# Quartered load of x, feed-forward weight scaling in the first attention, and the rotary addition on VectorE, in a two-layer transformer kernel

## The reference

```python
x = x + attn0(layernorm(x))   # 16 heads of 16, causal; rotary positions on q and k
x = x + ffn0(layernorm(x))    # layernorm again, sign(weight) product, then * max|weight| * gamma + beta
x = x + attn1(layernorm(x))   # 16 heads of 128, causal, with biases
x = x + moe(layernorm(x))     # 64 experts, 6 per token, capacity 96, plus a shared expert
```

## Time and profile before

| what | value |
|---|---|
| median of 3 runs | 1561.48 us |
| lowest, highest | 1559.58, 1565.09 us |
| span of the profiled execution, first to last instruction | 1556.1 us |
| busy in the span: PE, DVE, ACT, POOL | 1394.1, 1047.9, 814.5, 374.1 us |
| mean granted TensorE clock | 0.948 of full speed |

### The profile page before, as it was taken

How to read it: one execution, slowest core, us unless ns; L and a number is a source line. 1 busy time by engine, 2 the same in 40 slices (tenths; PEclk the granted TensorE clock), 3 DMA queues, 4 the chain that set the end, 5 groups by cost and what they waited for, 6 DMA issues and landing times. The chain is left out here.

```text
span 1556.1 us, 36410 instructions
## 1 busy us (share of the span) xinstructions
PE 1394.1 (90%) x12869; PEld 982.9 (63%) x12869; DVE 1047.9 (67%) x2191; ACT 814.5 (52%) x1682; POOL 374.1 (24%) x796
## 2 busy tenths in 40 slices
PE   3848999999679999999989999999998798799977
PEld 2414555554556777777777677777767745599963
DVE  4856777764778888888822888888882378422228
ACT  1316665655327877777711877787770116222330
POOL 0434665530021111111110101111101000577730
PEclk9969999999889999999999999999999799799985
DMA  3038999872025655565620665566651430599948
GB/s 101 1 68 170 248 246 248 214 160 52 1 79 113 143 138 138 133 142 133 138 59 1 129 141 134 135 142 138 138 128 31 133 95 1 162 290 288 289 135 295
DMA packets 463401, 215.08 MB, mean 138 GB/s; under 512 B 412082, under 2 KB 434448, under 8 KB 463072
## 3 DMA queue, kind: packets, MB, share of 16 engines
q1 hardware_dynamic: 448992, 175.09, 47.0%
q0 software_dynamic: 12000, 36.90, 8.0%
q10 hardware_dynamic: 2336, 2.16, 0.4%
HBM read 81.97 MB, written 31.52 MB: 73 GB/s over the span
## 5 line engine op out<-in xcount | busy, mean ns | idle before, releaser
L1073 PE MATMUL bank<-a_pt,v_part 128*128 128x128 f16 x3456 | 235.3, 220 | 13.9 <-DMA a_pt<-a_ph 8.9
L1136 ACT ACTIVATE a_ph<-a_p,a_rinv 128x1024 f16<-128x1024 f32 (+7 forms) x256 | 198.7, 777 | 79.3 <-POOL a_rinv L1015 75.7
L755 DVE TENSOR_REDUCE a_qh<-bank 128x1 f16<-128x1024 f32 (+7 forms) x256 | 182.3, 755 | 85.0 <-PE bank L645 83.3
L1073 PEld LDWEIGHTS bank<-a_pt,v_part 128*128 128x128 f16 x3456 | 208.9, 98 | 47.2 <-DVE z_part L1163 7.5
L1144 DVE TENSOR_REDUCE a_negm<-bank 128x1 f32<-128x1024 f32 (+7 forms) x256 | 191.7, 749 | 55.9 <-PE bank L1057 55.7
L1052 PE MATMUL bank<-a_k,a_q 128*128 128x512 f16 (+3 forms) x1152 | 228.7, 326 | 0.2
L743 ACT ACTIVATE a_p<-bank 128x1024 f32<-128x1024 f32 (+7 forms) x256 | 157.8, 649 | 128.7 <-PE bank L700 113.3
L1178 DVE SCALAR_TENSOR_TENSOR a_ph<-a_p,a_rinv,a_ph 128x1024 f16<-128x1024 f32 (+7 forms) x256 | 206.8, 808 | 1.7 <-ACT a_ph L1136 1.7
L1125 ACT ACTIVATE a_p<-bank,a_negm 128x1024 f32<-128x1024 f32 (+7 forms) x256 | 189.3, 739 | 21.6 <-DVE a_negm L1144 21.6
L1015 POOL TENSOR_TENSOR a_rinv<-a_rinv,p_scale 128x1 f32<-128x1 f32 x256 | 48.8, 191 | 610.6 <-DVE a_rinv L1157 610.4
L924 PE MATMUL bank<-x_part,wsplit 128*128 128x512 f16 x768 | 186.0, 379 | 4.1 <-PEq L199 1.8
(11 more groups left out here) (206 smaller groups left out, 2230.9 us busy)
## 6 DMA issues: line engine op xcount, KB each, us to landing
wgu<-in_wgu SPq DMA_DIRECT2D x64, 352.0 KB
choice_rows<-zero POOLq DMA_DIRECT2D x24, 512.0 KB, 4.9
c_rows<-choice_rows SPq DMA_DIRECT2D x16, 768.0 KB, 11.2
wsplit<-w_parts POOLq DMA_DIRECT2D x30, 384.0 KB, 3.8
wd<-in_wd SPq DMA_DIRECT2D x64, 176.0 KB
pw_in<-in_wqkv SPq DMA_DIRECT2D x16, 384.0 KB, 4.9
w_parts<-pw_part SPq DMA_DIRECT2D x16, 384.0 KB, 2.9
a_pt<-a_ph SPq DMA_TRANSPOSE x256, 3.0
```

The costliest lines, as they stand in the source:

```text
L755: dve.tensor_reduce(qh[s][:, i, MC:MC + 1], s1_place(t), AX.X, ALU.max, negate=True).then_inc(m_ready, 1)
L1073: ins = eng.matmul(Z_ps[:, cols], g.vs[par][v_][:, k, :], turned[slot][:, a * blocks[j] + k, :], start=(k == 0 and (v_, a) == PARTS[0]), s ...
L1136: eng.activation(parts[slot][:, 0:w_], probs[slot][:, 0:w_], ACT.Copy, scale=rinv[:, p_, jj:jj + 1]).then_inc(p_hi, 1)
```

## The change

- x is loaded in four transfers of four tiles, each with its own semaphore, and DVE takes the statistics of a quarter's tiles as soon as that quarter has landed, in `load` instead of `norm`.
- The transfers of the attention's and the feed-forward sublayer's weights are issued in `load`, behind those of x; SP waits for them in `norm`.
- POOL no longer takes part in `l0_qkv`: the rotary addition is DVE's, behind `low` of the tile before.
- The maximum over the partitions and the two multiplications that give `wf` are POOL's, at the end of its list in `l0_attention`. Gamma and the maximum move to buffers that live longer.
- The buffer of zeros is half as large, and each transfer of zeros reads it twice.
- The semaphores of the norms' chains are shared between the norms, with counts that go on.

```diff
 def load(nc, g, weights):
     s_x = [g.sem(f"ld_x{q}") for q in range(XQ)]          # XQ = 4
...
-                sp.dma_start(g.x[:, :, :], g.t["x"].rearrange("b (n p) d -> p (b n) d", p=P)).then_inc(s_x, 16)
+                xv = g.t["x"].rearrange("b (n p) d -> p (b n) d", p=P)
+                for q in range(XQ):
+                    tiles = slice(q * NT // XQ, (q + 1) * NT // XQ)
+                    sp.dma_start(g.x[:, tiles, :], xv[:, tiles, :]).then_inc(s_x[q], 16)
+                weights(sp)
...
-                dve.wait_ge(s_x, 16)
+                for t in range(NT):
+                    if t % (NT // XQ) == 0:
+                        dve.wait_ge(s_x[t * XQ // NT], 16)
+                    dve.bn_stats(g.stats[:, t, :], g.x[:, t, :]).then_inc(s_st, 1)
                 dve.wait_ge(s_v, 3)
...
 def norm(nc, g, tag, kind, loads=None, pool_work=None):
-                if tag == "n0":
-                    for t in range(NT):
-                        dve.bn_stats(st[:, t, :], g.x[:, t, :]).then_inc(s_st, 1)
...
 def ffn_weights(g, c):
-    def all_reduce(pool):
+    def scaled(pool):
         pool.wait_ge(s_ab, 1)
         pool.partition_all_reduce(am[:, 1:2], am[:, 0:1], P, bass.bass_isa.ReduceOp.max).then_inc(s_all, 1)
-    def scaled(dve):
-        dve.wait_ge(s_all, 1)
-        dve.tensor_scalar(gam[:, :], gam[:, :], am[:, 1:2], None, ALU.mult).then_inc(s_scale, 1)
-        dve.wait_ge(s_scale, 1)
-        dve.wait_ge(s_sg, 1)
-        dve.tensor_tensor(g.wf[:, :, :], g.wf[:, :, :], gam[:, :].unsqueeze(1).to_broadcast([P, DC, D]), ALU.mult)
+        pool.wait_ge(s_all, 1)
+        pool.tensor_scalar(gam[:, :], gam[:, :], am[:, 1:2], None, ALU.mult).then_inc(s_scale, 1)
+        pool.wait_ge(s_scale, 1)
+        pool.wait_ge(s_sg, 1)
+        pool.tensor_tensor(g.wf[:, :, :], g.wf[:, :, :], gam[:, :].unsqueeze(1).to_broadcast([P, DC, D]), ALU.mult)
...
 def l0_qkv(nc, g, sign, absmax):
                     if t >= 1:
                         low(t - 1)
+
+                    dve.wait_ge(s_rot, t + 1)
+                    dve.tensor_tensor(r[:, 0, :], r[:, 0, :], r[:, 1, :], ALU.add).then_inc(s_add, 1)
                 low(NT - 1)
-                scaled(dve)
-
-            @block.gpsimd
-            def _(pool):
-
-                all_reduce(pool)
-                for t in range(NT):
-                    pool.wait_ge(s_rot, t + 1)
-                    r = rot[t % 2]
-                    pool.tensor_tensor(r[:, 0, :], r[:, 0, :], r[:, 1, :], ALU.add).then_inc(s_add, 1)
...
 def l0_attention(nc, g, ffn_scaled, w_begin, w_split, w_load, w_store):
-                zv = g.krows.rearrange("(z p n) d -> z p (n d)", p=P, z=ZD)
+                zv = g.krows.rearrange("(z p a n) d -> z p a (n d)", p=P, z=ZD, a=2)
...
-                        pool.dma_start(zv[m - 4], g.zero[:, :]).then_inc(g.s_zero, 16)
+                        pool.dma_start(zv[m - 4], g.zero[:, :].unsqueeze(1).to_broadcast(
+                            [P, 2, K * T * D // P // ZD // 2])).then_inc(g.s_zero, 16)
                 for m in (NH - 2, NH - 1):
                     fetch_values(m)
+                ffn_scaled(pool)
```

More of the change, by code:

```diff
@@ L104, in build @@
         g.stats = sb("stats", [P, NT, 6])
-        g.zero = sb("zero", [P, K * T * D // P // ZD])
+        g.zero = sb("zero", [P, K * T * D // P // ZD // 2])
         g.xrows = nc.dram_tensor("token_rows", (T, D), F32, kind="Internal").ap()
@@ L112, in build @@
         g.mean = sb("mean", [P, NT])
-        load(nc, g)
         with ExitStack() as cx:
@@ L119, in build @@
                 with ExitStack() as cw:
[L120 to L123, removed]
+                    l0_loads, l0_loaded = l0_buffers(nc, g, c0, cw)
+                    ffn_loads, ffn_loaded, sign, absmax, scaled = ffn_weights(g, cw)
+                    load(nc, g, lambda sp: (l0_loads(sp), ffn_loads(sp)))
+                    norm(nc, g, "n0", None, lambda sp: (l0_loaded(sp), ffn_loaded(sp)))
+                    l0_qkv(nc, g, sign, absmax)
                 with ExitStack() as cw:
-                    l0_attention(nc, g, *l1_weights(g, cw))
+                    l0_attention(nc, g, scaled, *l1_weights(g, cw))
                 proj_out0(nc, g)
@@ L135, in build, with load @@
         moe(nc, g, out)
-def load(nc, g):
-    s_x, s_c, s_v = g.sem("ld_x"), g.sem("ld_const"), g.sem("ld_cast")
+def load(nc, g, weights):
+    s_c, s_v, s_st = g.sem("ld_const"), g.sem("ld_cast"), g.sem("n_stats")
+    XQ = 4
+    s_x = [g.sem(f"ld_x{q}") for q in range(XQ)]
     with ExitStack() as c:
@@ L168, in norm @@
 def norm(nc, g, tag, kind, loads=None, pool_work=None):
-    s_sq, s_ch = [g.sem(f"{tag}_{n}") for n in ("sqrt", "chain")]
+    s_sq, s_ch = [g.sem(f"n_{n}") for n in ("sqrt", "chain")]
+    SQ0, CH0 = {"n0": (0, 0), "n1": (1, 8), "n2": (3, 25), "n3": (4, 33)}[tag]
     s_st, s_ag, s_xn, s_tr = [g.sem(f"n_{n}") for n in ("stats", "aggr", "xn", "tr")]
@@ L226, in _ @@
             def _(dve):
-                n = 0
+                n = CH0
                 def chained(ins):
@@ L247, in _ @@
                     chained(dve.tensor_scalar(ve, t1, EPS, None, ALU.add))
-                    dve.wait_ge(s_sq, lv + 1)
+                    dve.wait_ge(s_sq, SQ0 + lv + 1)
                     chained(dve.reciprocal(sq[:, :], sq[:, :]))
@@ L283, in _ @@
                 for lv in range(levels):
-                    act.wait_ge(s_ch, 3 if lv == 0 else 11)
+                    act.wait_ge(s_ch, CH0 + (3 if lv == 0 else 11))
                     act.activation(sq[:, :], ve, ACT.Sqrt).then_inc(s_sq, 1)
@@ L331, in ffn_buffers @@
     g.beta = g.sb("beta", [P, D], F32, c)
+    g.gam = g.sb("fw_gamma", [P, D], F32, c)
+    g.am = g.sb("fw_am", [P, 2], F32, c)
 def ffn_weights(g, c):
@@ L336, in ffn_weights @@
     w = g.sb("fw_w", [P, DC, D], F32, c)
-    gam = g.sb("fw_gamma", [P, D], F32, c)
-    am = g.sb("fw_am", [P, 2], F32, c)
+    gam, am = g.gam, g.am
     def loads(sp):
@@ L345, in loads, with loaded @@
         sp.dma_start(g.lnb[:, :], g.t["ln_b"]).then_inc(s_in, 16)
+    def loaded(sp):
         sp.wait_ge(s_in, 80)
@@ L352, in absmax @@
         dve.tensor_reduce(am[:, 0:1], w[:, :, :], AX.XY, ALU.max, apply_absolute_value=True).then_inc(s_ab, 1)
-    def all_reduce(pool):
+    def scaled(pool):
         pool.wait_ge(s_ab, 1)
         pool.partition_all_reduce(am[:, 1:2], am[:, 0:1], P, bass.bass_isa.ReduceOp.max).then_inc(s_all, 1)
-    def scaled(dve):
-        dve.wait_ge(s_all, 1)
-        dve.tensor_scalar(gam[:, :], gam[:, :], am[:, 1:2], None, ALU.mult).then_inc(s_scale, 1)
-        dve.wait_ge(s_scale, 1)
-        dve.wait_ge(s_sg, 1)
-        dve.tensor_tensor(g.wf[:, :, :], g.wf[:, :, :], gam[:, :].unsqueeze(1).to_broadcast([P, DC, D]), ALU.mult)
-    return loads, sign, absmax, all_reduce, scaled
+        pool.wait_ge(s_all, 1)
[3 more added lines that the diff above has]
+        pool.tensor_tensor(g.wf[:, :, :], g.wf[:, :, :], gam[:, :].unsqueeze(1).to_broadcast([P, DC, D]), ALU.mult)
+    return loads, loaded, sign, absmax, scaled
 def l0_buffers(nc, g, c0, c):
@@ L384, in loads, with loaded, l0_qkv @@
         sp.dma_start(g.wo0[:, :, :], g.t["wo0"].rearrange("(c p) n -> p c n", p=P)).then_inc(s_in, 16)
+    def loaded(sp):
         sp.wait_ge(s_in, 48)
-    return loads
-def l0_qkv(nc, g, sign, absmax, all_reduce, scaled):
+    return loads, loaded
+def l0_qkv(nc, g, sign, absmax):
     w, rope = g.w0, g.rope
@@ L474, in _, with l0_attention @@
                     ins.then_inc(s_hi, 1)
-def l0_attention(nc, g, w_begin, w_split, w_load, w_store):
+def l0_attention(nc, g, ffn_scaled, w_begin, w_split, w_load, w_store):
     NH = B * H
```

## The result

The changed kernel takes 1542.68 us (median of 4, 1539.46 to 1545.0), the kernel before in the same comparison 1562.57 (median of 4). The ratio is 0.9877 with an interval of 0.9856 to 0.9899, so the change saves 1.2%, 19 to 20 us; 1541.1 was predicted, with 1538 to 1550 as the range. The profiled execution after has a span of 1537.8 us and a time of 1539.46, the lowest of the four. Time and span differ by 1.66 there; if they did before, the profiled execution before took some 1557.8 (an estimate), also less than any of its kernel's four runs (1559.58 and more).

The account below looks back on a forecast made before the run. PE is busy for most of the span, so time is won where PE stands still, mainly the first 92 us. Savings 3.9 + 15.3 + 1.1 = 20.4 from 1561.5 give 1541.1 us, range 1538 to 1550.

Parts of the forecast that it names:

- Front: Load of x: statistics of twelve tiles lie under x's landing, saving 3.93 us if x lands when it did.
- Rival 1: Load of x: quarters land late, paying for themselves or sharing the queue with the weights; 1544.7 to 1552.3 us; chance 0.10.
- The stall and the pace: `l0_qkv`: POOL's stall goes and a tile takes 2.65 us in place of 3.19; 15.3 us saved.
- Rival 2: `l0_qkv`: DVE is the bound and a tile stays at 3.19 us; 1549.2 us in all; chance 0.09.
- ACT's copy: `l0_qkv`: `low` waits 0.87 us for ACT's float16 copy of the tile before, hidden behind 1.28 of multiplications.
- The end: End of `l0_qkv`, from the last tile's multiplication to the next block: 4.55 us in place of 5.68, saving 1.1.
- POOL's tail: First attention: POOL's reduction and products behind its last copy end at about 382.0, 9.7 us to spare, costing nothing.
- Rival 4: End of first attention: POOL's code loading takes far longer, so the wait is moved, not hidden; 1556 to 1561 us; chance 0.04.
- Zeros: First attention: reading the halved source twice costs nothing; upper end 32 us of engine time.
- Rival 3: First attention: transfers of zeros slow it by up to 32 us, 1573 us in all; chance 0.05.
- one sign of a wrong forecast: First attention: longer than 300 us from its first POOL instruction to its last on DVE.
- The clock: `l0_qkv`: granted clock had fallen to 0.81 in the stall; PE has no such gap after the change, costed at nothing.

Follow-up runs that it names:

- the kernel with the readers: The changed kernel with 30 additions on POOL in `l0_qkv` that read two SBUF arrays and that nobody waits for; 1557.31 us, one run.
- the scale moved alone: Kernel before with only the reduction and two products moved to POOL's list end in the first attention, zeros halved, additions still on POOL; 1552.15 us, ratio 0.9928.
- the longer tail: The changed kernel with 17 more multiplications of gamma by 1.0 on POOL at the attention's end; 1547.97 us, ratio 0.9905.

## Why the prediction was right

- **Front: right, 0.2 too high.** 3.70 against 3.93 at the aggregation. The assumption that x lands when it did was off by what lacks: the last quarter lands at about 10.5, not 10.22. The rows bear out that the fixed parts overlap. The batching rule that the prediction weighed (the Trainium skill, DMA: Bandwidth & Descriptors, Bandwidth) speaks against quarters; here they landed within 10.5 - 1.8 = 8.7 us, where the estimate from the Trainium skill's page, which has its figures from transfers that GpSimd issues, was 12.8. Rival 1, x landing 3.6 late or more, fell with it, although eleven transfers did follow the first quarter.
- **The stall and the pace: right in kind, 1.1 too low.** The prediction took a tile as 2.65, with DVE as the bound; it is 2.58, and PE is the bound. The term that was mis-sized is the addition: costed at its length, 0.69, it adds 0.60 on a DVE that waits for nobody, as the two ends overlap (the kernel with the readers, behind their end). That is the other end that the prediction named, 0.61, and with it DVE needs 2.54 and PE's 2.57 decides. Fifteen tiles by 0.07 are 1.05. Rival 2, a pace that stays at 3.19, is out: it holds only while POOL's additions run beside DVE, as the scale moved alone and the readers show. ACT's copy, costed at nothing behind 1.28 of multiplications, shows no wait except ahead of the last `low`, where 0.87 was counted and 0.86 came.
- **The end: right.** 4.52 against 4.55.
- **POOL's tail: right.** 15.94 long against 15.9, 9.67 to spare against 9.7, and the longer tail shows that the slack is real. Rival 4, loading that takes far longer there, is out: 6.11 and 7.16 of idle time stand ahead of the reduction and of the first product, against 6.0 and 7.4 in the middle of `l0_qkv`.
- **Zeros: right.** Nothing, alone (1.0001) and in the change. Rival 3 fell: the zeros land no later, and the attention is 0.33 longer, not 32. By the letter one sign of a wrong forecast did appear, an attention longer than 300 us: it is 300.35. The sign was set too close, since the kernel before has 300.02 itself, and the repeat of the changed kernel has 299.66.
- **The clock: right where it was put, but not for the whole.** "I cost the clock at nothing" holds in `l0_qkv` of the changed kernel, at 1.00 from end to end. But the first tile was slow in three of the other kernels (1.6 us), so that it was not in this profile is luck, and the output projection gave 1.2 back, as it did, or more, in every kernel whose attention starts earlier. The prediction looked for the clock in `l0_qkv` alone. This and the spread of later stages are why the 20.87 us at the attention's end arrive as 18.3 in the span.

By the profiled executions the errors add up: 20.4 predicted, 1.1 more from the pace, 0.2 less from the front, 0.3 less from a longer attention and 2.6 less behind it make 18.4, and the span is 18.3 shorter. The medians of the comparison are 19.9 apart, only 0.5 less than predicted; that it is so close is luck, as the 1.1 more of the pace stands against what was lost behind the attention. The other 1.1 between 1541.1 and 1542.68 comes from the kernel before, whose median was 1561.48 when the prediction was made and is 1562.57 with a fourth run. The 5.4 that the prediction set between median and span isn't one thing: some 1.7 is what a time has over its span, and the rest is that the profiled execution lay below its kernel's median. What the prediction did not say is how the gains depend on one another. It priced the scale and the addition together; the runs show that the addition on DVE has nearly all of it, and that the move of the scale adds about 1 us.

## What to carry to other kernels

A reduction on POOL, with a change of its configuration ahead and another behind, cost 6.0 and 7.4 us here, but only to those queued behind it: before such an instruction is moved, look whether the queue behind it can be emptied instead. Where an instruction is slow only beside another engine's work, giving that work to the engine that seems full can shorten its list, as with 0.60 more and 1.06 less per tile here. When one engine's list gets shorter, look which engine bounds next: here PE, whose 2.58 lie just above DVE's 2.54. Parts that remove the same wait must be priced together and then each alone, since their gains do not add.

## What was not expected of the hardware

- Behind a POOL instruction a block took 2.29 us to hand over to the next, behind DVE's 0.30. One profile shows it.
- The granted clock fell for a few microseconds at places that are not the same from execution to execution: 0.83 and 1.00 in the same stretch of the same code, 2.4 us apart in span; and 0.57 at the first tile of `l0_qkv` in one kernel and 1.00 there in the changed kernel. The first tile's 1.6 us came in three kernels of this study; what decides is open.
- The 64 products of the output projection took 17.3 us in both kernels whose attention starts near 92 us, and 18.5 to 19.5 in the eleven profiles in which it starts earlier. Why is open.
- Beside POOL's additions `low` took 1.82, with one addition per tile (the scale moved alone) as with additions without a break; with the latter DVE's own addition grew as much, from 0.69 to 1.75.
